# Output bias added tile by tile, two projections moved ahead of the first maxima, the others moved between a tile's score products

## What is computed

```python
xn = _layernorm(x, axis=-1)
# attention: 16 heads of 16, one shared key and value head, rotary on 8 dims,
# causal window of 64 keys
q, k, v = xn @ Wq, xn @ Wk, xn @ Wv          # then apply_rope on q and k
scores = einsum('bhqd,bkd->bhqk', q, k) * scale + mask
attn = softmax(scores, axis=-1)
attention = (attn @ v) @ Wo + bo
# experts: router picks 4 of 64 experts per token, plus two shared experts
logits = xn @ router_w
_, topk_idx = top_k(logits + router_bias, 4)
routed = sum over the 4 chosen e of gate * (silu(xn @ wg[e]) * (xn @ wu[e])) @ wd[e]
shared = sum over 2 of (silu(xn @ swg) * (xn @ swu)) @ swd
out = x + attention + routed + shared
```

## Time and profile before

| what | value |
|---|---|
| median of 3 runs | 434.47 us (432.95 to 434.75) |
| profiled execution | 432.2 us |
| span of the profile | 430.9 us, so 1.3 us lie around it |
| mean granted TensorE clock | 0.952 |
| TensorE busy | 372.1 us (86%) |
| VectorE busy | 300.5 us (70%) |
| ScalarE busy | 218.2 us (51%) |
| GpSimd busy | 230.1 us (53%) |

### The profile page before, as it was taken

The page is one execution under the profiler, slowest core; times in us unless marked ns, Lnnn a source line. Parts: engine busy times, 40 slices in busy tenths (PEclk is TensorE's granted clock), DMA queues, the critical chain, the costliest instruction groups (busy, mean ns, idle before and its releaser), DMA issues.

```text
span 430.9 us, 9082 instructions
## 1 busy us (share of the span) xinstructions
PE 372.1 (86%) x2580; PEld 299.8 (70%) x2580; DVE 300.5 (70%) x946; ACT 218.2 (51%) x522; POOL 230.1 (53%) x383
## 2 busy tenths in 40 slices
PE   6969687888787698888999999999999959999954
PEld 3866454655454465567889999988888738888642
DVE  4998777877787568545877778777773164767666
ACT  1463776787586475365467776766662011111100
POOL 5495676888888641112333334443425666667650
PEclk9997899999898889999999999999999969999986
DMA  8860346645425528959977773587743323444331
GB/s 242 175 128 2 88 115 159 173 125 145 142 90 151 147 77 208 268 174 245 278 213 215 230 218 134 165 268 232 239 148 93 108 85 101 123 122 123 98 110 49
DMA packets 86753, 66.83 MB, mean 155 GB/s; under 512 B 43261, under 2 KB 82429, under 8 KB 86705
## 3 DMA queue, kind: packets, MB, share of 16 engines
q1 hardware_dynamic: 80145, 49.28, 41.4%
q0 software_dynamic: 6144, 16.79, 12.7%
q10 hardware_dynamic: 416, 0.18, 0.3%
HBM read 36.75 MB, written 29.23 MB: 153 GB/s over the span
## 4 chain that ended last, share of the span: by engine, by line
PE 52%; DVE 17%; another core or an unknown queue 12%; issue 8%; ACT 6%; DMA 4%; SPq 1%; DVEq 0%; ACTq 0%
PE bank L592 12%; PE bank L576 12%; PE bank L525 6%; PE bank L550 4%; PE bank L535 4%; PE bank L451 2%; DVE xall L1183 2%; PE bank L388 2%; PE bank L372 2%; PE bank L476 2%; PE bank L432 2%; DVE xall L949 2%; ACT xall L722 2%; ACT xall L739 2%
## 5 line engine op out<-in xcount | busy, mean ns | idle before, releaser
L1136 DVE SCALAR_TENSOR_TENSOR spare<-bank,halfmask,spare 64x128 f32<-64x128 f32 x254 | 90.1, 355 | 31.4 <-ACT spare L783 28.5
L1337 POOL COPY spare<-wall 128x256 f32 x127 | 50.4, 400 | 104.0 <-PE bank L576 91.3
L1383 POOL DMA_INDIRECT wall<-y_d,y_row x64 | 61.7, 965 | 38.3 <-issue 15.8
L592 PE MATMUL bank<-wdn,spare 128*128 x254 | 78.1, 390 | 3.6 <-DVE spare L1136 1.9
L576 PEld LDWEIGHTS bank<-xall,spare 128*128 128x128 f32 x508 | 76.3, 191 | 6.9 <-issue 0.5
L1319 POOL DMA_INDIRECT xs_d<-spare,slot_i x64 | 64.1, 1002 | 26.0 <-issue 9.1
L576 PE MATMUL bank<-xall,spare 128*128 x508 | 76.9, 275 | 0.3 <-ACT xall L773 0.3
L525 PE MATMUL bank<-xnT,xall 128*128 128x256 f32 x256 | 58.9, 384 | 1.1 <-issue 0.7
L525 PEld LDWEIGHTS bank<-xnT,xall 128*128 128x128 f32 x256 | 49.2, 193 | 9.1 <-issue 1.5
L758 ACT ACTIVATE xall<-bank 128x256 f32<-128x256 f32 x32 | 11.6, 382 | 81.4 <-remote 43.6
L791 ACT ACTIVATE spare<-bank 128x256 f32<-128x256 f32 x106 | 40.6, 383 | 21.9 <-PE bank L592 19.1
(11 more groups left out here) (160 smaller groups left out, 562.6 us busy)
## 6 DMA issues: line engine op xcount, KB each, us to landing
y_d<-spare SPq DMA_DIRECT2D x127, 128.0 KB, 2.7
wall<-in_wg SPq DMA_DIRECT2D x16, 256.0 KB, 4.9
wall<-in_wu SPq DMA_DIRECT2D x16, 256.0 KB, 5.1
wdn<-in_wd SPq DMA_DIRECT2D x8, 512.0 KB, 5.9
spare<-xs_d SPq DMA_DIRECT2D x32, 128.0 KB, 2.7
small<-xs_d SPq DMA_DIRECT2D x32, 128.0 KB, 2.7
wall<-in_x SPq DMA_DIRECT2D x4, 512.0 KB, 5.9
base_d<-spare SPq DMA_DIRECT2D x16, 128.0 KB
```

The lines of the kernel that those rows point to most:

```text
L592: pe.matmul(y_bank(i), hT[i % NB], wdn[:, bass.ds(o, D)], start=True, stop=True).then_inc(s["down"], 1)
L1136: ins = dve.scalar_tensor_tensor(hT[i % NB][half], u, halfmask[half, i:i + 1], sg[i % NB][0:F], ALU.mult, ALU.mult)
L1337: pool.tensor_copy(wcur[i % NW], wall[:, bass.ds(o, WE)]).then_inc(s["weights"], 1)
L1383: pool.indirect_dma_start(out=yk[:, T, k, :], out_offset=None, in_=y_d, in_offset=bass.IndirectOffsetOnAxis(ap=y_row[:, T, k:k + 1], axis= ...
```

## The change

GpSimd adds the bias in 16 instructions of one tile each instead of four of four tiles each, and VectorE waits for its own tile's. TensorE projects tiles 4 and 5 behind the last logits, ahead of `stack_k(1)` and the first maxima, and tiles 6 and 7 stay where they were. In turns 1 to 7 the tile that was projected behind the second maxima is now projected behind the first two score products (turns 2 to 7, tiles 10 to 15) or behind the third (turn 1, tile 9). ScalarE copies tile 4 ahead of the first copy of the logits and tile 5 behind the cast of tile 1. In the later turns it takes the exponentials of both first parts before it copies a projected tile and before `attention`; this last move holds for all turns, also those without a projection.

```diff
-    LATE_TILES = (((4,), (5,), (6,), (7,)), ((8,), (), (9,), ())) + tuple(((), (), (t,), ()) for t in range(10, NT))
+    AHEAD = (4, 5)
+    LATE_TILES = (((), (), (6,), (7,)), ((8,), (), (), (9,))) + tuple(((), (), (t,), ()) for t in range(10, NT))
@@ tensor
         logits(NT - 1)
+        for t in AHEAD:
+            project(t)
         stack_k(1)
@@ tensor, loop over T
             maxima(T, 1)
-            for t in late_tile(T, 2):
-                project(t)
             if T == 0:
+                for t in late_tile(T, 2):
+                    project(t)
                 totals()
                 for i in range(2):
                     rank(i)
             if T:
                 scores(T - 1, 0, 0)
                 scores(T - 1, 0, 1)
+            if T:
+                for t in late_tile(T, 2):
+                    project(t)
             if T > 1:
                 attention(T - 2)
             if T:
                 scores(T - 1, 1, 0)
+                for t in late_tile(T, 3):
+                    project(t)
             place(T)
             if T:
                 scores(T - 1, 1, 1)
-            for t in late_tile(T, 3):
-                project(t)
+            else:
+                for t in late_tile(T, 3):
+                    project(t)
@@ scalar
+        copy_qk(AHEAD[0])
         copy_logits(0)
         cast(1, 2)
+        copy_qk(AHEAD[1])
         copy_logits(1)
@@ scalar, loop over T
+            if T:
+                scores(T - 1, 0, 0)
+                scores(T - 1, 0, 1)
             for t in late_tile(T, 2):
                 copy_qk(t)
-            if T:
-                scores(T - 1, 0, 0)
             if T > 1:
                 attention(T - 2)
             if T:
-                scores(T - 1, 0, 1)
                 scores(T - 1, 1, 0)
@@ vector
-            dve.wait_ge(s["x_bo"], b + 1)
+            dve.wait_ge(s["x_bo"], T + 1)
@@ gpsimd
-        for b in range(B):
-            pool.wait_ge(s["normed"], (b + 1) * TPB)
-            pool.tensor_tensor(x_in[b], x_in[b], bo_sb.unsqueeze(1).to_broadcast([P, TPB, D]), ALU.add).then_inc(s["x_bo"], 1)
+        for T in range(NT):
+            b, t = divmod(T, TPB)
+            if t == 0:
+                pool.wait_ge(s["normed"], (b + 1) * TPB)
+            pool.tensor_tensor(x_in[b][:, t, :], x_in[b][:, t, :], bo_sb, ALU.add).then_inc(s["x_bo"], 1)
```

## The result

The changed kernel takes 436.05 us in the median of 19 runs, beside 434.32 us for the kernel before on the same chip in the same sitting. The ratio is 1.0072, 95% interval 1.0047 to 1.0098. I forecast 430.7; it is slower by 0.7%. The profiled execution took 436.46 us (span 435.2, mean granted clock 0.954); the one before took 432.2 (430.9, 0.952).

The account below looks back on a forecast made before the run. No engine was taken as the bound throughout, so edits were priced where they stand. First turn 1.0, turn 1 0.2, turns 2 to 7 2.0, turns 8 to 15 0.6: 3.8 us off 434.47, giving 430.7, range 427.5 to 434.2.

Parts of the forecast that it names:

- Bias tile by tile: Loop's start: VectorE waits only for a short GpSimd addition, not a whole long one; 2.5 us gained.
- Tiles 4 and 5 ahead, and the new pause: First turn: projections hidden, but a 2.3 us TensorE pause likely lowers the clock; first turn's gain 1.0, bounds 0 and 2.5.
- Turn 1: Tile 9 fills a pause ahead of `place`, its copy leaves the exponentials' front: 0.2 us, bounds 0 and 0.4.
- Turns 2 to 7: Exponentials no longer wait for the projection; ScalarE's waits ahead of copies and `attention` go: 2.0 us, bounds 0.8 and 2.8.
- the third product behind the projection: Turns 2 to 7: ScalarE reaches this product only behind copy and `attention`, so its delay is hidden.
- Turns 8 to 15: The second exponential runs in ScalarE's 1.1 us wait ahead of `attention`: 0.6 us, bounds 0 and 1.1.
- what the loop saves reaches the end whole: Behind the loop: later steps start from its end by semaphores, not at a fixed time, so its saving should stay whole.
- GpSimd rival: GpSimd bounds turns 5 to 8, new order does nothing there, or the split has no effect: 432.5 us; chance 0.10.
- slower rival: Shifted start of the last stage makes two more unexplained ScalarE waits: 440.3 us, one more 435.5; chance 0.08.
- if another wait grows by what the copies lose: Test on the profile after, turns 2 to 7: the forecast is wrong if another wait takes up the copies' vanished wait.

Follow-up runs that it names:

- start: Kernel before with the bias added tile by tile and tiles 4 and 5 projected ahead, old order in the turns: 0.9984, on another chip 0.9974.
- C: Kernel before with only the new order of turns 1 to 15, tile 9's move included: 404.17 against 402.16 us, 1.0059.
- E: GpSimd's 64 scatters spread otherwise over the turns; added to the start 0.9940, to the changed kernel 0.9976 of the kernel before.
- D: `place` transposed into bank 0, not the small bank; changed kernel with it 0.9965 and 0.9942 of the kernel before, kernel before with it 0.9980.
- A: Kernel before with only the bias added tile by tile: 401.15 against 403.23 us, 0.9943; together with C, D and E 0.9921.

## Why the prediction was wrong

*Bias tile by tile: right in mechanism, near in size.* The first L1035 took 0.90 and the first L935 0.50 us, where I had 1.0 and under 1.3 as the test. An addition took 0.72 in the median, between my bounds of 0.59 and 0.82. This part alone is 0.9943, 2.1 us of 403, where I had 2.5 before the clock's share.

*Tiles 4 and 5 ahead, and the new pause: right, and it should have been a warning.* The pause was 2.77 us where I had 2.3, the clock fell at its end, and the first turn won 0.88 for my 1.0. That the number fits so well is partly luck: I took half a loss as a mean, and the clock fell in six of twelve profiles. But 2.5 without the projections and 1.0 with them is a sum that speaks against the projections. They bring nothing elsewhere that is seen: start 0.9974, bias alone 0.9943. I priced the loss and did not ask what it buys.

*Turn 1.* Forecast 0.2. The lead was 0.9 at the end of the first turn and in turn 1 (47.1 for 48.0), and 0.3 in turn 2, where after had a stall of 1.65 us that nothing on the core ends. So no gain is seen.

*Turns 2 to 7: this step failed.* I took 2.0, bounds 0.8 and 2.8, from ScalarE's waits ahead of the copies. They went to zero, and the turns did not get shorter by as much: 0.4 to 1.0 us on the 402 us chips, while in the profile of after they got 1.0 longer, a lead of 0.3 us in turn 2 that became a lag of 0.7 in turn 7. What I missed is that ScalarE's attention copy is not only work of ScalarE. It is also what frees the small bank for `place`. I asked who waits in front of the moved copy, and not who waits for it. The code says it (`small_reader`), and the trace of before has the wait once, 0.9 us, in the row shown above. With the bank out of the way the turns are 3.1 us shorter than the start's on the 402 us chips, a little over my upper bound of 2.8: the gain of the order was there, and the hidden wait took most of it. Half of the missing piece was named, as I had the third product behind the projection; the fourth, behind `place`, I did not follow.

*Turns 8 to 15: failed likewise.* I took 0.6 from the wait of 1.1 us ahead of `attention`. It fell to 0.2, and that ahead of the exponentials grew from 1.1 to 2.6. After lagged by 0.7 in turn 7 and by 4.5 in turn 8, and ended the stack copies 2.8 late. The step in turn 8 is a stall of 6.16 us that nothing on the core ends, with a mean granted clock of 0.71 from 106 to 120 us (before: 0.88); before had one of 2.55 in the same place, and one of 5.25 later. The four of after make 15.0 us, the three of before 11.5. I can't say that the change makes them longer: on another of the slower chips after had 5.9 in two, and the ratio there was 1.0016 (0.9986 to 1.0045), below the whole interval of the result (1.0047 to 1.0098); a 402 us chip gave 1.0011. So of the 0.7% on the chip of the result, the greater part may come from these stalls, and its size stays open. The part that repeats is C against the start: 2.6 and 1.7 us on two 402 us chips; the 0.9 us with E on a 430 us chip is not clear of the noise.

*The sum and what follows from it.* That what the loop saves reaches the end whole failed too, on the 402 us chips. I took the end of the loop for the end of the turns, while on the 402 us chips GpSimd's stream of scatters and rotations paces it. With D the changed kernel's turns are 3.1 us shorter than the start's, and its last scatter is 0.75 us earlier (152.05 for 152.80), or 0.2 (152.60) in the profile in which the clock fell as in the start's; with A, C, D and E the last copy of `stack` is 5.2 us earlier than with A alone, and the last scatter not at all.

*The rivals.* The GpSimd rival (0.10) named the right engine for the 402 us chips; on the chip of the result no cast of ScalarE waits over 1 us for GpSimd. It had the new order pay nothing in turns 5 to 8, and at worst left the rest of the gain standing. It failed in that it priced the spare only: 2.9 us in front of one cast. I didn't ask whether the change would make GpSimd itself slower, though the same mechanism, an engine held for the whole of another's instruction, stood in my own first part. The slower rival (0.08) had the right sign and the wrong place, the last stage, where the stalls were 39.7 for 43.6; those in the loop it did not price. What makes these stalls is shown by no run. The case that happened, a wait that takes the place of the one removed, was among my tests ("if another wait grows by what the copies lose"), but had no chance and no price. (By its own terms the slower rival's 440.3 is 440.4.)

The range ended at 434.2, and the time was 436.05. It had no case in which the turns lose.

## What to carry to other kernels

When an instruction is moved back in an engine's queue, list everything that its completion releases, buffers and PSUM banks too, and what is queued behind each of those waits on the other engines; a wait of its own engine that vanishes says nothing about them. Check which stream really paces a loop: add up what each engine waits for the others in it (GpSimd 2.4 to 5.5 of 106 to 110 us here), and look again on another chip, since GpSimd had 12% of the chain on one and none on another. Split a long instruction that other engines are seen to wait for, and look in the trace of before at which pairs start close together, because a shift of a few tenths of a microsecond can make them collide.

## What the runs showed of the hardware

An indirect DMA issued by GpSimd, 1.0 us alone, took 1.79 to 2.03 us when it started 0.1 to 0.4 us behind a VectorE operation of 128x1024 with two inputs in SBUF. In all twenty profiles, fifteen scatters started 0.06 to 0.63 us behind such an operation; they took 1.44 to 2.03 us and ended 0.83 to 0.89 us after it, as if almost the whole of each had waited. One that started 0.2 us ahead took 1.01, and the VectorE step beside it its usual 1.23. Beside a reduction of 128x1024 with a single input, a scatter that started 0.4 us behind it took 0.99.

A pause of TensorE of 2.76 or 2.77 us inside `totals` was followed by the low clock in six profiled executions and not in six others; pauses of 1.74 to 1.75 us in the same place were not in three.

Chips differ in the whole program by 6.5 to 8% (429.6 and 434.3 us against 401.7 to 403.2 for the kernel before): on the faster ones, the waits that nothing on the core ends are absent, where the profile before has 11.5 us of them on ScalarE in the turns and 43.6 in the last stage. What they are is not known from these runs.
